# Turning six quantised weight units as a sum of an fp32 and a bf16 product, with a new order, in a gated cross-attention and FP8 feed-forward kernel

## The reference, cut to what matters

```python
def _fp8(x):
    return x.astype(jnp.float8_e4m3fn).astype(jnp.float32)
def _qlinear(qx, scale_x, scale, W, idx, out_idx=None):
    Wr = W[:, idx]
    w_scale = jnp.max(jnp.abs(Wr), axis=1, keepdims=True) / FP8_MAX
    qw = _fp8(Wr / w_scale)
    y = qx * scale_x @ (qw * w_scale).T * scale
    ...
x = x + jnp.tanh(g_xattn[0]) * _L0_xattn_ref(_layernorm(x, axis=-1), ctx_512, ...)
x = x + jnp.tanh(g_ffn[0]) * _L0_ffn_ref(_layernorm(x, axis=-1), w_gate, w_up, w_down, ...)
```

## Time and profile before

| | |
|---|---|
| median of 3 runs | 728.0 us (727.83 to 728.09) |
| the profiled execution | 729.19 us, span of its instructions 727.4 us |
| busy: TensorE, VectorE, ScalarE, POOL | 657.9, 680.1, 555.5, 538.5 us |
| granted TensorE clock, mean | 0.978 |

### The profile page before, as it was taken

The page is one execution under the profiler, slowest core; times in us unless marked ns, Lnnn a source line. Parts: engine busy times, 40 slices in busy tenths (PEclk is TensorE's granted clock), DMA queues, the critical chain, the costliest instruction groups (busy, mean ns, idle before and its releaser), DMA issues.

```text
span 727.4 us, 15637 instructions
## 1 busy us (share of the span) xinstructions
PE 657.9 (90%) x6091; PEld 419.9 (58%) x6160; DVE 680.1 (93%) x1127; ACT 555.5 (76%) x995; POOL 538.5 (74%) x601
## 2 busy tenths in 40 slices
PE   1758698999999999999999999999999999998794
PEld 1647476666566666566565657566566556545342
DVE  4999998989899999999999999999999999999997
ACT  6896878987869787878878787979797867555642
POOL 6768889796968778687878686968696677666651
PEclk9888999999999999999999999999999999999997
DMA  8887768385795757585867566675775686512121
GB/s 303 223 153 199 157 147 176 80 176 94 123 158 107 152 105 154 80 181 96 167 108 141 111 144 116 132 144 114 155 123 116 90 150 100 111 22 87 27 70 58
DMA packets 143479, 93.57 MB, mean 129 GB/s; under 512 B 107598, under 2 KB 114126, under 8 KB 143406
## 3 DMA queue, kind: packets, MB, share of 16 engines
q1 hardware_dynamic: 141246, 90.74, 61.6%
q0 software_dynamic: 576, 1.45, 0.8%
q10 hardware_dynamic: 1584, 0.39, 0.3%
HBM read 31.59 MB, written 9.83 MB: 57 GB/s over the span
## 4 chain that ended last, share of the span: by engine, by line
PE 47%; DVE 29%; POOL 11%; DMA 5%; issue 3%; ACT 3%; SPq 0%; ACTq 0%; DVEq 0%
PE pair L1153 26%; DVE mx L3116 5%; POOL PT L793 4%; PE pair L1411 4%; PE pair L1416 3%; DVE room L2943 2%; DVE room L2947 2%; PE pair L1394 2%; DVE room L3260 2%; PE pair L1440 2%; DVE room L3308 2%; PE pair L1436 2%; POOL room L832 2%; DVE tm L3323 2%; DVE wmax L2962 2%
## 5 line engine op out<-in xcount | busy, mean ns | idle before, releaser
L832 POOL TENSOR_TENSOR room<-room,up_scale 128x512 f32<-128x512 f32 (+1 forms) x96 | 125.6, 1312 | 63.1 <-ACT room L2349 62.2
L3116 DVE TENSOR_REDUCE mx<-pair 128x6 f32<-128x768 f32 x128 | 117.6, 947 | 1.7 <-PE pair L1343 1.4
L793 POOL TENSOR_SCALAR_AFFINE_SELECT PT<-PT 128x512 f32<-128x512 f32 x128 | 104.0, 841 | 13.1 <-ACT PT L2274 13.0
L2274 ACT ACTIVATE PT<-pair 128x768 f32<-128x768 f32 x128 | 98.3, 814 | 9.4 <-PE pair L1394 7.8
L1153 PE MATMUL pair<-WgT,room 128*128 128x512 bf16 (+1 forms) x382 | 89.5, 366 | 2.5 <-DVE room L3447 0.8
L1153 PE MATMUL pair<-xT,WqTh 128*128 128x256 bf16 x512 | 86.5, 272 | 1.5 <-ACT WdT L2037 1.3
L1153 PE MATMUL pair<-WuT,room 128*128 128x512 bf16 (+1 forms) x368 | 84.8, 361 | 3.3 <-DVE room L3260 1.4
L2349 ACT ACTIVATE room<-room,sx 128x512 f32<-128x512 f32 (+1 forms) x96 | 65.2, 682 | 24.2 <-DVE room L3260 18.8
L1153 PE MATMUL pair<-WdT,room 128*128 128x512 bf16 x326 | 75.4, 379 | 3.1 <-DMA room<-room 2.9
L2381 ACT ACTIVATE room<-room 128x512 bf16<-128x512 f32 (+1 forms) x96 | 55.8, 586 | 21.2 <-DVE room L3308 21.1
L1153 PE MATMUL pair<-xT,WqTl 128*128 128x256 bf16 x256 | 69.7, 272 | 0.0
(11 more groups left out here) (151 smaller groups left out, 1863.4 us busy)
## 6 DMA issues: line engine op xcount, KB each, us to landing
xin<-in_x_dram SPq DMA_DIRECT2D x16, 512.0 KB, 4.0
x<-in_x_dram SPq DMA_DIRECT2D x16, 512.0 KB, 4.8
K<-kh SPq DMA_DIRECT2D x32, 256.0 KB, 4.9
Q<-qh SPq DMA_DIRECT2D x32, 256.0 KB, 4.6
out_dram<-x SPq DMA_DIRECT2D x15, 512.0 KB, 3.0
K<-kl SPq DMA_DIRECT2D x16, 256.0 KB, 6.1
Q<-kl SPq DMA_DIRECT2D x16, 256.0 KB, 4.2
room<-in_L_ffn_w_down_dram SPq DMA_DIRECT2D x4, 704.0 KB, 9.0
```

The lines of the kernel that those rows point to most:

```text
L793: pool.affine_select(out=view, in_=view, compare_op=ALU.is_ge, fill=0.0, base=0, pattern=[[0, 2], [0, 2], [1, P]], channel_multiplier=-1). ...
L832: pool.tensor_tensor(g, g, up_scale[:, chunk(n)[1]], ALU.mult).then_inc(slw_done, 1)
L2274: act.activation(head_columns(ring(b, c), 0, 384), head_columns(shifted_pair[c][:, :], 0, 384), ACT.Exp, scale=SCALE).then_inc(exp_done, 1)
L3116: dve.tensor_reduce(mx[:, heads, :], head_columns(w, 0, 3 * P).rearrange("p h (r s) -> p h r s", s=P), AX.X, ALU.max).then_inc(max_done, 1)
```

## The change

The six units 4, 6, 8, 10, 12 and 14 lose their `unit_rounded` pass. VectorE's scaling step now subtracts the lift instead of adding it, which rounds in the same way, and leaves the difference in the fp32 raw tile. TensorE then adds the lift while it turns: an fp32 product of the raw tile with the identity opens the sum in PSUM, a bf16 product of `q` with the identity closes it. Since the sum is fp32, it takes two banks of PSUM in place of one. A buffer of the ring is free only when its unit has been turned, so the loads of units 8, 10, 12 and 14 wait for `w_turned`. All else of the diff is a new list of calls on every engine, new PSUM banks, and the waits that go with them; the same steps are called otherwise.

```diff
+TURNED_APART = (4, 6, 8, 10, 12, 14)
@@ unit_bank
+            if u in TURNED_APART:
+                return pairs[w_bank[u] // 2][:, 0:KT * k * P]
@@ unit_loaded (SyncE)
                 if u == 8:
-                    sp.wait_ge(w_round_dve, 5)
+                    sp.wait_ge(w_turned, 5)
                 if u == 10:
-                    sp.wait_ge(w_round_dve, 6)
+                    sp.wait_ge(w_turned, 6)
                 if u == 12:
-                    sp.wait_ge(w_round_dve, 7)
+                    sp.wait_ge(w_turned, 10)
                 if u == 14:
-                    sp.wait_ge(w_round_dve, 8)
+                    sp.wait_ge(w_turned, 9)
@@ unit_turned (TensorE)
-                        last = pe.transpose(w[:, (i * k + m) * P:(i * k + m + 1) * P], q_tile(u, m)[:, tok(i)], identb[:, :])
+                        here = w[:, (i * k + m) * P:(i * k + m + 1) * P]
+                        if u in TURNED_APART:
+                            pe.matmul(here, raw_tile(u, m)[:, tok(i)], ident[:, :], start=True, stop=False)
+                            last = pe.matmul(here, q_tile(u, m)[:, tok(i)], identb[:, :], start=False, stop=True)
+                        else:
+                            last = pe.transpose(here, q_tile(u, m)[:, tok(i)], identb[:, :])
@@ unit_lifted (VectorE)
-                                                    in1=q_tile(u, m), op0=ALU.mult, op1=ALU.add)
+                                                    in1=q_tile(u, m), op0=ALU.mult,
+                                                    op1=ALU.subtract if u in TURNED_APART else ALU.add)
@@ the list of VectorE
-            unit_rounded(8)
-            unit_rounded(10)
...
```

More of the change, by code:

```diff
@@ L1638, in _ @@
             scores(1, 7)
+            spread(4)
+            projected(0, 1)
             queries(2, 0)
+            turned_maxima(1)
             queries(2, 1)
-            projected(0, 1)
-            turned_maxima(1)
             queries(2, 2)
+            queries(2, 3)
             projected(0, 2)
@@ L1646, in _ @@
             shifted(1, 1)
-            queries(2, 3)
+            projected(0, 3)
             shifted(1, 2)
-            projected(0, 3)
             shifted(1, 3)
+            shifted(1, 4)
             values(2, 0)
-            shifted(1, 4)
             shifted(1, 5)
@@ L1712, in _ @@
             down(0, 0)
+            scores(3, 0)
             up_products(1, 0)
-            scores(3, 0)
+            scores(3, 1)
             gate_products(1, 0)
-            scores(3, 1)
             scores(3, 2)
             projected(2, 0)
+            keys(4, 0)
+            keys(4, 1)
+            scores(3, 3)
+            scores(3, 4)
             projected(2, 1)
-            keys(4, 0)
-            scores(3, 3)
-            keys(4, 1)
-            scores(3, 4)
+            queries(4, 0)
             gate_products(1, 1)
@@ L1824, in _ @@
             scores(12, 7)
+            queries(13, 1)
             up_products(10, 1)
+            up_products(10, 2)
             gate_products(10, 3)
[L1827 to L1829 removed]
             turned_maxima(12)
             queries(13, 2)
+            gate_products(10, 4)
             queries(13, 3)
@@ L1992, in _ @@
             projected(15, 2)
+            projected(15, 3)
             gate_products(14, 1)
-            projected(15, 3)
             gate_products(14, 2)
+            gate_products(14, 3)
             up_products(14, 1)
-            gate_products(14, 3)
             up_products(14, 2)
@@ L2441, in _ @@
+            unit_abs(6)
+            unit_taken(1)
+            queries_high(0, 0)
+            values_taken(0, 1)
+            x_high(1, 0)
+            x_normal(1, 0)
+            attention_weights_exact(6)
+            attention_weights_high(6)
+            queries_exact(0, 1)
+            queries_high(0, 1)
+            x_high(1, 1)
+            attention_weights_high(7)
+            x_normal(1, 1)
+            unit_abs(5)
+            unit_abs(4)
+            attention_weights_exact(7)
             unit_taken(0)
-            unit_taken(1)
+            unit_taken(3)
@@ L3656, in _ @@
                 up(k, 5)
+                floored_x(k + 1, 1)
                 rounded_x(k + 1, 0)
                 largest_t(k, 1)
-                largest_t_inverted(k, 1)
+                lifted_x(k + 1, 1)
                 sums_inverted(k + 2)
@@ L3852, in _ @@
             up(12, 3)
+            lifted_t(12, 0)
+            rounded_t(12, 0)
             up(12, 4)
-            rounded_t(12, 0)
+            floored_x(13, 1)
             lifted_x(13, 0)
-            maxima(15, 0)
-            floored_x(13, 1)
+            lifted_x(13, 1)
             rounded_x(13, 0)
-            lifted_x(13, 1)
             rounded_x(13, 1)
@@ L3904, in _ @@
             floored_x(14, 0)
+            up(13, 4)
             up(13, 5)
+            lifted_x(14, 0)
             largest_t(13, 1)
-            lifted_x(14, 0)
             rounded_x(14, 0)
             sums_inverted(15)
+            floored_x(14, 1)
             inverse_spread(15, 0)
```

2661 lines of the change are left out of this document (1360 added, 1301 removed).

## The result

The changed kernel took **737.4 us** (median of 4 runs, 736.4 to 738.5), the kernel before beside it 728.05. The ratio is 1.0129, with a 95% interval from 1.0111 to 1.0146: 9.4 us slower, where 5.4 us faster was forecast. It lies outside the range, on the side that had a chance of 0.12, and above the slowest rival (730.3).

What follows compares the result with a forecast made beforehand. VectorE was taken to pace set-up and tail, TensorE the middle. Terms -9.6 (passes) + 3.2 (products) + 1.0 (other engines) = -5.4 us gave a 722.6 us median, range 718.5 to 728.5.

Steps and rivals of the forecast that it cites:

- the slowest rival (730.3): Loop: the new order makes TensorE wait for a maximum, 0.7 us a period, 7.7 us in all; chance 0.12.
- Since VectorE is full wherever they stood, nothing hides them: -9.6: Set-up: removing six VectorE subtractions of 128x1024 starts the middle 9.6 us earlier.
- gave it 1 us: Set-up: POOL, ScalarE and TensorE not passing on all of VectorE's gain, SyncE's share included, costs +1.0 us.
- So 0.20 us each: Set-up, TensorE: each of 48 added fp32 matmuls takes 0.20 us near the full clock, 9.7 us together.
- These 6.4 us are hidden by TensorE waiting for VectorE: Set-up: fp32 products of units 4, 6, 8 and 10, 6.4 us (at most 13), fall into TensorE's idle time.
- +3.2: Set-up at about 122 us: 16 fp32 products of units 12 and 14 add 3.2 us on the path.
- The middle: I take 0: Loop: same steps in a new order; a period can win 0.3 us at most, or lose more; taken as 0.
- The stalling loop: Loop: one more 0.9 us step delays maximum 5, a period costs 0.7 us more, total 730.3 us; chance 0.12.
- that margin: Loop: maximum 5 is ready after 5.4 us, TensorE wants it for scores 7 after 5.6: 0.2 us to spare.
- VectorE's busy time: Whole kernel, sign of being right: VectorE's six passes are gone and its busy time is down by about 9.6 us.
- SyncE and late buffers: Set-up: unit 12's later load costs nothing to 2 us; as a rival, 2 us late, 724.6 us, chance 0.04.

Runs made afterwards that it cites:

- with plain DMAs: Changed kernel with its 92 transposing DMAs replaced by plain ones of the same blocks, transposition left out: 732.5 us; kernel before with the same replacement: 728.3 us.

## Why the prediction was wrong, point by point

*"Since VectorE is full wherever they stood, nothing hides them: -9.6."* The first step that failed. VectorE was busy for 19.8 of 20 us, yet the passes were worth 1.9 us in the old order. A full engine shows that nothing can be added, not that what is taken away is won. The scores that its maxima wait for, the absolute values of ScalarE and the gate weights' DMA came just in time, and each took a part as a wait: VectorE's waits rose from 4.3 to 8.1 us. The set-up's chain in the earlier trace rows showed as much: from 74.5 to 90.4 us it ran over a queue, two DMAs and POOL. The prediction read it as a danger to the later part only and gave it 1 us.

*"So 0.20 us each."* The second. The earlier trace rows has eight records in 1.62 us; they were four products, since an fp32 product leaves two records. A product adds 0.28 us at the full clock, 0.53 at half. The kernel's own counts would have told: 26 products of `spread` stand for 52 records of that line.

*"These 6.4 us are hidden by TensorE waiting for VectorE."* The third, and the dearest. The products stand directly ahead of scores in TensorE's order, and the idle time of the window lay elsewhere in it: a window's idle time hides only what is ready when the engine idles. So the products made the scores late and VectorE waited for them, 8.5 us where it had waited 1.1; the prediction had VectorE as the one waited for. Unit 4 fell into a stretch at a clock of 0.50 and took 5.2 us in all. Leaving out the products of units 4 to 10 gave 3.8 us; in the old order, with the passes cut, all products cost 6.6. The term *+3.2* for units 12 and 14 was 0.5.

*"The middle: I take 0."* The fourth. The period went from 38.47 to 39.14 us. The stalling loop was a rival, with a period 0.7 us longer, and 0.67 came, on top of the loss in the set-up. That the size agrees is luck: it was worked out for scores 7 and maximum 5, and that margin held, as no scores of TensorE wait for a maximum from 210 to 510 us. The text had argued from TensorE and VectorE alone. It had not laid the distance between POOL's two writers of `kl` beside the DMA that reads it in between: `keys_low(k + 4, 1)` moved behind `up_scaled` 1 to 3, and in SyncE's queue a strip of the queries now goes ahead of the low keys. What makes the period 0.17 us longer with plain DMAs was not tested.

*VectorE's busy time.* It was to fall by 9.6 and rose by 0.5. One form explains most of it, `lifted_T` in the kernel before and after, whose number and size are the same:

```profile
L3364 DVE SCALAR_TENSOR_TENSOR room<-room,tmult 128x1408 f16<-128x1408 f32 x30 | 52.6, 1753 | 0.1
```

```profile
L3464 DVE SCALAR_TENSOR_TENSOR room<-room,tmult 128x1408 f16<-128x1408 f32 x30 | 60.0, 2000 | 0.4
```

7.4 us more for the same 30 instructions: in the new order one of the two per period runs 2.51 us, beside POOL's `up_scaled` for its first 1.0 us and beside `var_eps` for the last 1.4. `var_eps` works on 128x2 elements and took 0.19 us in the kernel before; here it takes 1.46 and stands in the chain of the period (340.29 above). What that costs was not tested. The prediction used this contention (a POOL subtraction of 2.4 us in place of 1.2) only as something that the removed passes would free, and not as something that a new order can add. The Trainium skill, SBUF — State Buffer, "Who interferes with whom", has an instruction with two SBUF inputs on VectorE and a reading one on GpSimd exclude each other; the 2.51 against 1.75 us, and the 1.46 against 0.19, agree with it.

*SyncE and late buffers.* Unit 12 was no problem, as forecast; its load and maximum caused no wait of VectorE.

The sum as it was, in medians: the passes and the new order without the products end at 728.2, so 0 in place of -9.6 + 1.0; the products +4.3 in place of +3.2; the loop and the tail with the transposing DMAs +5.0 in place of 0. Together +9.3 of the 9.4 measured; it adds up because each term is the step from one run to the next, not because each was found by itself. Of the 5.0, the traces have 3.5 us by the start of `down(9, 0)`, which is the loop. The other 2 us, in the tail, come in two places by the trace: TensorE waits 1.0 us more at 607.0 for the second transposing DMA of `xT` (5.35 us from issue to landing), and at 661.1 it waits for the DMA `Q<-mT`, where with plain DMAs no DMA is in the chain. No run tested these. No version of the changed order beat the kernel before: with the products free of charge, it only reaches it.

## What to carry to other kernels

An engine that is busy all the time need not set the pace: before you book the time of work removed from it, look who feeds it at the end of that stretch and how late that comes; cutting the work to a few columns in the old order tells what it is worth. Count the records of an operation against the number in the code before dividing. Where a new order moves a step that overwrites a buffer, compare the distance between its last writer and the next one with what the DMA between them takes, its place in the queue included: here 11.8 us became 8.9 with a DMA that needs nearly 10, and that cost 3.5 to 4 us over the loop. And compare an engine's matmuls with its weight loads before you read its busy time: 69 missing ones made a rise of 11 us look like 18.

## What the runs showed of the hardware that was not expected

- An fp32 product of 128x128 by 128x128 leaves two records and adds 0.28 us to a bf16 product at a clock of 1.00, while four fp32 transposes (line 1167) took 0.61 us at 56.8 us, 0.15 each, at a clock of 0.73 in the mean.
- TensorE stood idle for 2.41 us up to 49.53 in the changed kernel, and its granted clock was 0.50 from 50.3 to 57.1 us. The pair that costs 0.33 us later cost 0.64 there.
- A transposing DMA held SyncE's queue for 1.20 us per issue (`qxT`) and 1.41 (`qtT`) in the changed kernel's loop (medians), a plain one of the same blocks for 0.60 and 0.61. To landing they took 2.9 and 3.9 us, the plain ones 2.4 and 3.8. The longer issue ahead of the low keys is half of what made these late (0.5 us); their own DMA took 0.4 us more to land.
- The low keys' DMA moved behind one 256-KB transfer made each period 0.7 us longer, through POOL's wait of 1.3 us for it.
- A VectorE instruction of 2.51 us stretched a GpSimd step on 128x2 elements from 0.19 to 1.46 us.
